# A burst of forty identity transpositions ahead of the first tokens, and token tiles transposed one by one as they are normalised

## The chip, the cores and the metric

One Trainium2 chip, one core of it. The metric is the device time of one execution in microseconds (us), median of the runs.

## What is computed

A graph-attention layer and a mixture-of-experts layer, each on layer-normalised tokens with a residual, over 16 batches of 512 tokens of 256 features in fp32. Cut to what matters:

```python
q, k, v = xn @ Wq.T, xn @ Wk.T, xn @ Wv.T          # xn = layernorm(x), 8 heads of 32
scores = where(adj != 0, q k^T / sqrt(32), -inf)
c = softmax(scores) @ v
gate = sigmoid(concat(c, xn) @ Wg.T + bg)
x = x + gate * xn + (1 - gate) * c
x = x + sum over the top 2 of 8 experts, and a shared expert, of (silu(y Wg) * (y Wu)) Wd     # y = layernorm(x)
```

## The kernel before, in words

**Two phases, one order of slots.** Attention runs first, the experts behind it; `seam` (L53) is the order of the work for TensorE, ScalarE and VectorE. Attention goes through iterations b = -1, 0, ..., 17 of 32 slots each. A slot is one score tile: one head's 128 queries against 512 keys. TensorE does the score matmul (L532, into one of two PSUM banks `S`), VectorE scales, masks and takes the row maximum (L916), ScalarE exponentiates (L677), TensorE transposes the result in four 128x128 tiles (L543), ScalarE or, in two slots of each 32, VectorE copies that to SBUF (L665, L908), and every eight slots TensorE multiplies by v (L576). Iteration b does the scores of batch b; between the slots' own work stand "units" of other batches' work, by the table `UNIT_AT` (L25).

**Units.** P0 and P1 (slots 18 and 19) transpose the normalised tokens of batch B = b+1: `turn` (L439) makes four transpositions of 128x128 (L441), one for each tile of 128 tokens, for one half of the features. ScalarE copies the bank to a rounded high part (`xt_h`, L605) and VectorE makes the rest (`xt_l`, L769). Q0 and K0 (slots 22, 23 and 24, 25, one half of the contraction in each) multiply by the weights, as three matmuls each time (`split`, L433: high x high, high x low, low x high; L435, L436, L437), and L611 and L772 take the result apart in the same way. Q1, K1, V0, V1 follow in the next iteration. A unit's bank is free again when the counter `g_free` says so; the units pass in one order, those that an iteration does not need being passed by with a bare increment.

**The start.** In iteration -1 there are no scores. SP issues the loads (L337 to L344: the tokens of batch 0, the weights; then the first half of the adjacency, L366). VectorE takes the statistics of batch 0, GpSimd the reciprocal deviation (L1032), and VectorE normalises tile by tile in `first_batch` (L748, L755), each of the four instructions counting `s_xn` up by one. For every later batch GpSimd does that (L1037), in slot 13 of the iteration before. TensorE's program begins with a wait for the constants that GpSimd writes (`s_const`, L431; the last is `tok_i`, L1003), the identity among them, and its first work is P0. The wait before a P unit asks for all four tiles:

```python
                if name[0] == "P":
                    pe.wait_ge(s_xn, B * NT + NT)
                    last = turn(o, xn, k)
```

ScalarE rounds both halves of the q, k, v weights (L646, L647) ahead of its copy of P0, and the gate's weights (L649) behind that of P1. VectorE makes the weights' low parts (`split_qkv`, L713), each ahead of the low part of P0 and of P1, then turns the first half of the adjacency into a mask (`scores_mask`, L745). SP waits for that mask, loads the second half of the adjacency into the same tile (L395), waits for K0's low part and then issues twelve copies of the heads' rows into `stack` (L332), the store of the normalised tokens (L426) and the next loads. VectorE turns the second half into a mask three slots behind K0, and only then passes by the last units of iteration -1. That frees the counter on which Q1, K1, V0 and V1 of batch 0 wait; TensorE does those four at the end of iteration -1 (L553), and VectorE copies V1 (L780), works through `prepare` (L716 to L737) and takes the first score tile. TensorE is two score tiles ahead and then waits for it.

Of the kernel before, what the change touches and what calls it, by code (L numbers as in the profile page):

```python
# [6 lines left out]
P = 128  # L7
# [18 lines left out]
           "Z3": 17, "P0": 18, "P1": 19, "Q0": 22, "K0": 24, "X0": 29, "X1": 30}  # L26
HALVES = "QKV"

ACT_AT = {"exp": 5}
TURNED_BY_VECTOR = (14, 22)  # L30
DVE_AT = {"choose": 3, "mark": 4, "weigh": 6, "place": 14, "stat": 12, "var": 12, "bias0": 4, "bias1": 16, "gate": (17, 19),
# [41 lines left out]
def attention_phase(nc, sems, held, banks, x, adj, wqkv, wgate, bg, router_w, xn_dram, x1_dram, xt2_dram, xg_dram,  # L73
# [8 lines left out]
    NT = N // P  # L82
# [17 lines left out]
    if True:  # L100
        def sb(name, shape, dt=F32):
            return held.enter_context(nc.sbuf_tensor(name, shape, dt))

        def sem(name):
            return sems.enter_context(nc.semaphore(name))

        S = banks[0:2]
# [10 lines left out]
        xn = sb("xn", [P, NT, D])  # L118
# [74 lines left out]
        s_xn = sem("s_xn")  # L193
# [78 lines left out]
        def late(b):  # L272

            return b >= 2 if isinstance(b, int) else True

        def unit(b, name):

            return (b + 1) * NU + ORDER.index(name)

        def bank(b, name):  # L280
            if b >= NB:
                return banks[(SEAM_BANKS if b == NB else LAST_BANKS)[name]]
            return G[unit(b, name) % 3]
# [39 lines left out]
        def first(b):  # L323

            return isinstance(b, int) and b == -1
# [103 lines left out]

        def tensor(pe):  # L430
            pe.wait_ge(s_const, 9)  # L431

            def split(out, lh, ll, rh, rl, first, last):  # L433

                pe.matmul(out, lh, rh, start=first, stop=False)  # L435
                pe.matmul(out, lh, rl, start=False, stop=False)  # L436
                return pe.matmul(out, ll, rh, start=False, stop=last)  # L437

            def turn(out, src, kf):  # L439
                for i in range(NT):  # L440
                    last = pe.transpose(out[:, P * i:P * i + P], src[:, i, P * kf:P * kf + P], ident[:, :])  # L441
                return last

            def do_unit(b, par, name, piece, end):
                B, A = b + 1, b - 1
                o = bank(b, name)
                k = int(name[1])
                s = par

                if piece == 0 and not (isinstance(b, int) and b == -1 and ORDER.index(name) < 2):  # L450
                    if b == NB + 1 and name != "R0":
                        pe.wait_ge(g_free, unit(NB, LAST_BEHIND[name]) + 1)
                    elif b == NB + 1:
                        pe.wait_ge(g_free, unit(b, LAST_BEHIND[name]) + 1)
                    elif b == NB and name in SEAM_BEHIND:
                        pe.wait_ge(g_free, unit(b, SEAM_BEHIND[name]) + 1)
                    elif b < NB:
                        pe.wait_ge(g_free, unit(b, name) - 2)
                    elif name == "L0":
                        pe.wait_ge(g_free, unit(b, name) - 1)  # L460
                if name[0] == "P":
                    pe.wait_ge(s_xn, B * NT + NT)
                    last = turn(o, xn, k)
                elif name[0] in "QK":
                    if first(b):
                        pe.wait_ge(s_lo, piece + 1)
                    if k == 0:
                        pe.wait_ge(g_free, unit(b, f"P{piece}") + 1)
                    xs = s if k == 0 else 1 - s
                    c0 = (D if name[0] == "K" else 0) + P * k  # L470
                    last = split(o[:, :], wqkv_h[:, piece, c0:c0 + P], wqkv_l[:, piece, c0:c0 + P],
                                 xt_h[xs][:, piece, :], xt_l[xs][:, piece, :], piece == 0, piece == KF - 1)
                elif name[0] == "V":
                    i = 2 * k + piece
                    for kf in range(KF):
                        last = split(o[:, D * piece:D * piece + D], xt_h[1 - s][:, kf, P * i:P * i + P],
                                     xt_l[1 - s][:, kf, P * i:P * i + P], wqkv_h[:, kf, 2 * D:],
                                     wqkv_l[:, kf, 2 * D:], kf == 0, kf == KF - 1)
                elif name[0] == "C":
                    pe.wait_ge(s_norm, A * 2 + 2)  # L480
                    last = turn(o, c_tok, k)
                elif name[0] == "Z":
                    if isinstance(b, int) and b == 1:
                        pe.wait_ge(s_set, 7)
                    tok = slice(P * k, P * k + P)
                    pe.matmul(o[:, 0:D], pick2[:, :], bg2[:, :], start=True, stop=False)
                    for kf in range(KF):
                        split(o[:, 0:D], xt_h[s][:, kf, tok], xt_l[s][:, kf, tok],
                              wg_h[:, KF + kf, :], wg_l[:, KF + kf, :], False, False)
                    for kf in range(KF):  # L490
                        pe.wait_ge(g_free, unit(b, f"C{kf}") + 1)
                        last = split(o[:, 0:D], ct_h[:, kf, tok], ct_l[:, kf, tok],
                                     wg_h[:, kf, :], wg_l[:, kf, :], False, kf == KF - 1)
                elif name[0] == "X":
                    pe.wait_ge(s_xn2, A * NT + NT)
                    last = turn(o, xn2, k)
                elif name[0] == "L":
                    zt = z[:, :, :].rearrange("p i d -> p (i d)")
                    for kf in range(KF):
                        pe.wait_ge(g_free, unit(b - 1, f"X{kf}") + 1)  # L500
                        for i in range(NT):
                            last = pe.matmul(o[DK * i:DK * i + DK, 0:P], rw_wide[:, kf, :],  # L502
                                             zt[:, N * kf + P * i:N * kf + P * i + P], start=kf == 0, stop=kf == KF - 1)
                elif name[0] == "M":
                    pe.wait_ge(g_free, unit(b, "L0") + 1)
                    last = pe.transpose(o[:, 0:P], lgt[:, :], ident[:, :])
                elif name[0] == "R":


                    pe.wait_ge(s_rt, (b - 2) * RT + RT_MB)  # L510
                    oe = o[:, 0:NT * E].rearrange("p (i e) -> p i e", e=E)
                    pe.matmul(oe, below[:, :], mb[:, :, :], start=True, stop=False)
                    for j in range(NT - 1):
                        pe.matmul(oe[:, j + 1:NT, :], ones_b[:, :],
                                  mb[:, j:j + 1, :].to_broadcast([P, NT - 1 - j, E]), start=False, stop=False)
                    last = pe.matmul(oe, ones_b[:, :], msum[:, :].rearrange("p (o e) -> p o e", o=1)
                                     .to_broadcast([P, NT, E]), start=False, stop=True)
                if end:
                    last.then_inc(g_full, 1)

            def at(b, p):
# [24 lines left out]
                for name, piece, end in pieces(b, p):  # L546
                    if has(b, name, att, pre, post):
                        do_unit(b, par, name, piece, end)
                    elif end:

                        pe.wait_ge(g_full, unit(b, name))
                        pe.nop().then_inc(g_full, 1)
                if first(b) and p == POS - 1:  # L553

                    par0, att0, pre0, post0 = flags(0)
                    for name in EARLY:
                        if has(0, name, att0, pre0, post0):
                            for piece in range(2):
                                do_unit(0, par0, name, piece, piece == 1)
                        else:  # L560
                            pe.wait_ge(g_full, unit(0, name))
                            pe.nop().then_inc(g_full, 1)
# [28 lines left out]
        def scalar(act):  # L591
# [44 lines left out]
            def second_choice(A):  # L636

                act.wait_ge(s_rt, A * RT + RT_DL)
                act.activation(el[:, :], dl[:, :], ACT.Exp).then_inc(s_el, 1)

            def at(b, p):
# [38 lines left out]
                if was and ep % 16 == 0:  # L680
# [5 lines left out]
                    act.activation(ct[g][:, :], C[:, :], ACT.Copy).then_inc(s_ct, 1)  # L686
                if p == ACT_AT["exp"] and late(b):
                    second_choice(b - 2)
# [299 lines left out]
        def pool(pool):  # L988
# [32 lines left out]
            def at(b, p):  # L1021
# [33 lines left out]
                if post and p == POOL_AT["xn2"]:  # L1055
# [11 lines left out]
                    for h in range(2):  # L1067
                        pool.tensor_copy(xs_half[:, :, XW * h:XW * h + D], xn2_half[:, :, :, h]).then_inc(s_halves, 1)
            return at, scatter

        return Attention(sync, tensor, scalar, vector, pool, unit, RT, s_done, t_free, t_full, pv, s_rt, g_full, g_free,
                         s_st, s_ref, s_xnst)

# [829 lines left out]
```

## Time and profile before

| what | value |
|---|---|
| runs | 1725.0, 1723.13 and 1724.4 us, median 1724.4 us |
| the profiled execution | 1724.81 us; its span from first to last instruction 1723.1 us |
| TensorE matmul busy | 1679.2 us, 97% of the span |
| VectorE, ScalarE, GpSimd busy | 1294.6, 1085.8 and 666.9 us |
| mean granted TensorE clock | 0.995 |

PE is TensorE's matmul side, PEld its weight load, DVE VectorE, ACT ScalarE, POOL GpSimd, SPq the issue of DMAs by SP. A line L441 is line 441 of the kernel. In the timeline a row has its start in us, its length in us (of several instructions together where it says x4), and in brackets how long the engine had been idle and what ended that.

### The profile page before, as it was taken

The page shows a single profiled execution, that of the slowest core. Times are in us where ns is not written, and L with a number is a line of the kernel's source. Part 1 is how long each engine was busy: PE and PEld are TensorE (multiplying, and loading weights), DVE is VectorE, ACT ScalarE, POOL GpSimd, SP SyncE. Part 2 cuts the span into 40 slices and gives each one's busy share as a digit, 9 for nine tenths or more (in the row PEclk, how much of TensorE's full clock was granted, in tenths as well). Part 3 has the DMA queues.
Part 4 walks back from the last instruction along what each step waited for, and adds up shares of the span by engine and source line. Part 5 has one row for each costly group of instructions (what it writes and reads, how often), then busy time and mean ns, then how long its engine had stood idle before and what let it go on. Part 6 is the DMA issues. An engine that isn't in the chain of part 4 may idle for free.

```text
span 1723.1 us, 35527 instructions
## 1 busy us (share of the span) xinstructions
PE 1679.2 (97%) x12185; PEld 1417.9 (82%) x12185; DVE 1294.6 (75%) x3220; ACT 1085.8 (63%) x2477; POOL 666.9 (39%) x512
## 2 busy tenths in 40 slices
PE   5999999999999999999999999999999999999997
PEld 4778888777887877887788888888898889888986
DVE  5688888888888888888555554777878787878784
ACT  4898888989888898988534333344444444434443
POOL 0146554456645445663331000034333443343334
PEclk9999999999999999999999999999999999999999
DMA  7355566656556665556333345587977786888773
GB/s 192 102 148 154 165 176 173 180 161 169 157 169 175 170 181 165 164 153 177 100 134 111 110 150 197 147 178 144 164 171 172 163 165 151 172 174 174 142 165 41
DMA packets 228081, 269.50 MB, mean 156 GB/s; under 512 B 107200, under 2 KB 184384, under 8 KB 222912
## 3 DMA queue, kind: packets, MB, share of 16 engines
q1 hardware_dynamic: 201312, 231.31, 50.2%
q0 software_dynamic: 26592, 35.93, 11.2%
q8 instruction: 99, 1.62, 0.4%
q14 instruction: 78, 0.64, 0.1%
HBM read 123.38 MB, written 74.86 MB: 115 GB/s over the span
## 4 chain that ended last, share of the span: by engine, by line
PE 45%; issue 1%; DVE 1%; DMA 1%; POOL 1%; ACT 1%; POOLq 0%; DVEq 0%; ACTq 0%
PE bank L1418 15%; PE bank L1420 15%; PE bank L1419 15%; DMA out_x<-yb,ix 1%; POOL out_x L1292 1%; DVE am L1587 0%; DVE wh L1547 0%; ACT ah L1513 0%; DVE xl L1578 0%; ACT yb L1501 0%; DVE al L1590 0%; ACT xh L1487 0%; PE bank L441 0%; DVE wa L1617 0%; PE bank L502 0%
## 5 line engine op out<-in xcount | busy, mean ns | idle before, releaser
L916 DVE CUSTOM_DVE_ANT_0 pf<-bank,bias_q 128x512 f32<-128x512 f32 x512 | 348.9, 687 | 130.2 <-PE bank L532 125.5
L1292 POOL DMA_INDIRECT out_x<-yb,ix x142 | 237.1, 1670 | 536.0 <-ACT yb L1501 409.9
L1513 ACT ACTIVATE ah<-am 128x512 fp32r<-128x512 f32 (+1 forms) x220 | 133.0, 605 | 424.7 <-DVE am L1587 424.7
L677 ACT ACTIVATE pf<-pf,nmax 128x512 f32<-128x512 f32 x512 | 373.7, 730 | 21.2 <-DVE nmax L916 21.2
L1418 PE MATMUL bank<-xh,wh 128*128 128x512 f32 (+1 forms) x880 | 334.4, 380 | 1.5 <-ACT pt L665 0.9
L1420 PE MATMUL bank<-xh,wl 128*128 128x512 f32 (+1 forms) x880 | 332.6, 378 | 0.0
L1419 PE MATMUL bank<-xl,wh 128*128 128x512 f32 (+1 forms) x880 | 332.5, 378 | 0.0
L543 PE MATMUL bank<-ident,pf 128*128 128x128 f32 x2048 | 312.6, 275 | 8.2 <-DVE pt L908 4.2
L543 PEld LDWEIGHTS bank<-ident,pf 128*128 128x128 f32 x2048 | 251.8, 141 | 64.6 <-issue 21.4
L665 ACT ACTIVATE pt<-bank 128x512 f32<-128x512 f32 x480 | 288.0, 600 | 10.3 <-PE bank L543 8.6
L1590 DVE TENSOR_TENSOR al<-am,ah 128x512 fp32r<-128x512 f32 (+1 forms) x220 | 146.7, 667 | 147.6 <-ACT ah L1513 147.6
L532 PE MATMUL bank<-stack 96*128 96x512 f32 x512 | 234.4, 458 | 5.8 <-DVE nmax L916 5.0
L1418 PE MATMUL bank<-wh,ah 128*128 128x256 f32 x824 | 232.6, 282 | 1.5 <-issue 1.5
L1420 PE MATMUL bank<-wh,al 128*128 128x256 f32 x824 | 232.6, 282 | 0.0
L1419 PE MATMUL bank<-wl,ah 128*128 128x256 f32 x824 | 232.6, 282 | 0.0
L1587 DVE TENSOR_TENSOR am<-sg,bank 128x512 f32<-128x512 f32 (+1 forms) x220 | 142.7, 649 | 81.6 <-PE bank L1420 78.0
L1418 PEld LDWEIGHTS bank<-xh,wh 128*128 128x128 f32 x880 | 165.5, 188 | 36.8 <-issue 3.8
L1420 PEld LDWEIGHTS bank<-xh,wl 128*128 128x128 f32 x880 | 165.3, 188 | 32.4
L1419 PEld LDWEIGHTS bank<-xl,wh 128*128 128x128 f32 x880 | 165.4, 188 | 29.8
L1017 POOL DMA_INDIRECT xg_dram<-xs,idx x128 | 132.9, 1038 | 107.8 <-DVE idx L892 60.9
L1511 ACT ACTIVATE sg<-bank 128x512 f32<-128x512 f32 (+1 forms) x220 | 124.2, 565 | 77.3 <-PE bank L1420 75.7
L1418 PEld LDWEIGHTS bank<-wh,ah 128*128 128x128 f32 x824 | 157.0, 190 | 3.6 <-issue 1.6
(209 smaller groups left out, 3050.6 us busy)
## 6 DMA issues: line engine op xcount, KB each, us to landing
raw<-in_w_all SPq DMA_DIRECT2D x39, 1536.0 KB, 7.5
stack<-qk SPq DMA_DIRECT2D x384, 128.0 KB, 2.4
adj_i<-in_adj SPq DMA_DIRECT2D x32, 512.0 KB, 4.7
xn<-in_x SPq DMA_DIRECT2D x16, 512.0 KB, 6.2
xn_dram<-xn SPq DMA_DIRECT2D x16, 512.0 KB, 2.9
xp<-in_x SPq DMA_DIRECT2D x16, 512.0 KB, 7.0
xnp<-xn_dram SPq DMA_DIRECT2D x16, 512.0 KB, 7.9
x_dram<-x SPq DMA_DIRECT2D x16, 512.0 KB, 3.2
```

The source lines that it names most:

```text
L532: pe.matmul(S[p % 2][:, :], stack[0:SR, hd, 0, P * tq:P * tq + P], stack[0:SR, hd, 1, :], start=True, stop=True).then_inc(s_full, 1)
L543: last = pe.transpose(T[ep % 2][:, P * kt:P * kt + P], pf[ep % RING][:, P * kt:P * kt + P], ident[:, :])
L665: act.activation(pt[r][:, j, :, P * (tq % 2):P * (tq % 2) + P], T[ep % 2][:, :].rearrange("p (k q) -> p k q", q=P), ACT.Copy).then_inc(t_f ...
L677: act.activation(pf[i][:, :], pf[i][:, :], ACT.Exp, bias=nmax[:, i:i + 1], scale=-1.0, accum_out=den[:, g, tq, j:j + 1]).then_inc(p_exp, 1)
L916: dve.tensor_tensor_reduce(pf[r][:, :], S[p % 2][:, :], bias_q[1 - par][:, tq, :], -SCALE, -3.0 * MASKED, ALU.add, ALU.min, nmax[:, r:r + ...
L1292: pool.indirect_dma_start(out=out, out_offset=bass.IndirectOffsetOnAxis(ap=ix[n % RING][:, i:i + 1], axis=0), in_=yb[s][:, i, :], in_offse ...
L1418: pe.matmul(out_, lh, rh, start=first, stop=False)
L1419: pe.matmul(out_, lh, rl, start=False, stop=False)
L1420: return pe.matmul(out_, ll, rh, start=False, stop=last)
L1513: act.activation(ah[s][:, m, 0:cols], am[m % 2][:, 0:cols], ACT.Copy).then_inc(s_ah, 1)
L1587: dve.tensor_tensor(am[m % 2][:, 0:cols], sg[m % 2][:, 0:cols], UB[m % 2][:, 0:cols], ALU.mult).then_inc(s_am, 1)
L1590: dve.tensor_tensor(al[s][:, m, 0:cols], am[m % 2][:, 0:cols], f32(ah[s][:, m, 0:cols]), ALU.subtract).then_inc(s_al, 1)
```

## The change

TensorE's program transposes the identity 40 times into the first score bank, once the constants are there and before anything else; the bank is written by the first score matmul later on. `turn` can take a start count: with it, each of the four transpositions of a P unit waits for its own tile of normalised tokens, not the first of them for all four. All P units of all batches are issued in this way. Nothing else differs.

```diff
+WARM = 40
...
         def tensor(pe):
             pe.wait_ge(s_const, 9)
+            for _ in range(WARM):
+                pe.transpose(S[0][:, 0:P], ident[:, :], ident[:, :])
...
-            def turn(out, src, kf):
+            def turn(out, src, kf, ready=None):
                 for i in range(NT):
+                    if ready is not None:
+                        pe.wait_ge(s_xn, ready + i + 1)
                     last = pe.transpose(out[:, P * i:P * i + P], src[:, i, P * kf:P * kf + P], ident[:, :])
                 return last
...
                 if name[0] == "P":
-                    pe.wait_ge(s_xn, B * NT + NT)
-                    last = turn(o, xn, k)
+                    last = turn(o, xn, k, B * NT)
```

## Rows read from the trace of the kernel before

**Rows 1.** Busy by stretch: us, then PE, PEld, DVE, ACT, POOL, granted clock, DMA share, GB/s
```profile
0.00:50.00 50.00, 30.16 (x171) 22.18 (x171) 31.56 (x87) 27.34 (x60) 9.14 (x21) 0.97 0.61 166
...
100.00:200.00 100.00, 99.14 (x881) 80.26 (x880) 82.93 (x266) 89.41 (x221) 45.81 (x37) 1.00 0.57 159
```

**Rows 2.** Timeline, the first 12 us: start, length, engine, line, operation, idle before
```profile
2.54 0.12 POOL L1003 IOTA tok_i<- 128x4 int32 x1
...
8.58 1.38 DVE L755 TENSOR_SCALAR xn<-xn,mv,rstd 128x256 f32<-128x256 f32 x4 [1.23 <-POOL rstd L1032]
...
10.10 0.83 ACT L647 ACTIVATE wqkv_h<-diff 128x768 fp32r<-128x768 f32 x1
10.11 1.94 PE L441 MATMUL bank<-ident,xn 128*128 128x128 f32 x8 [10.11 <-DVE xn L755]
...
11.23 0.60 ACT L605 ACTIVATE xt_h<-bank 128x512 fp32r<-128x512 f32 x1 [0.31 <-PE bank L441]
```

**Rows 3.** Timeline, 12 to 20 us, on TensorE, ScalarE, VectorE and SP
```profile
12.70 0.77 PE L435 MATMUL bank<-xt_h,wqkv_h 128*128 128x512 f32 x1 [0.65 <-DVE xt_l L769]
...
14.17 0.77 PE L435 MATMUL bank<-xt_h,wqkv_h 128*128 128x512 f32 x1
...
14.65 0.37 SPq L395 DMA_DIRECT2D adj_i<-in_adj  x1
...
15.58 0.63 PE L435 MATMUL bank<-xt_h,wqkv_h 128*128 128x512 f32 x1
...
16.01 0.56 PE L436 MATMUL bank<-xt_l,wqkv_h 128*128 128x512 f32 x1
...
16.64 0.40 PE L435 MATMUL bank<-xt_h,wqkv_h 128*128 128x512 f32 x1
...
17.11 0.39 PE L437 MATMUL bank<-xt_h,wqkv_l 128*128 128x512 f32 x1
...
18.16 0.69 DVE L772 TENSOR_TENSOR qk<-bank,qk 128x512 fp32r<-128x512 f32 x1 [1.02 <-ACT qk L611]
18.77 0.68 DVE L745 TENSOR_SCALAR bias_q<-adj_i 128x1024 bf16<-128x1024 int32 x1
...
19.10 0.50 PE L435 MATMUL bank<-xt_h,wqkv_h 128*128 128x512 f32 x1 [1.60 <-ACTq L634]
```

**Rows 4.** DMA issues of 14.7 to 18.5 us: KB each, us from issue to landing
```profile
adj_i<-in_adj SPq DMA_DIRECT2D x1, 512.0 KB, 3.3
```

**Rows 5.** Timeline, 25 to 30 us, on VectorE and TensorE
```profile
25.02 0.69 DVE L780 COPY v<-bank 128x512 f32<-128x512 f32 x1 [0.75 <-PE bank L437]
...
28.55 0.69 DVE L916 CUSTOM_DVE_ANT_0 pf<-bank,bias_q 128x512 f32<-128x512 f32 x1 [0.36 <-DVE bg L733]
...
29.39 0.47 PE L532 MATMUL bank<-stack 96*128 96x512 f32 x1 [3.94 <-DVE nmax L916]
```

**Rows 6.** Busy by stretch again, columns as in the first group
```profile
10.10:12.10 2.00, 1.94 (x8) 1.55 (x8) 1.20 (x2) 1.44 (x4) 0.00 (x0) 1.00 0.03 9
29.90:33.30 3.40, 3.24 (x12) 2.73 (x13) 2.41 (x9) 3.28 (x10) 0.00 (x0) 0.52 0.71 226
33.30:50.20 16.90, 13.35 (x102) 9.06 (x101) 13.19 (x40) 16.05 (x41) 6.29 (x5) 1.00 0.59 141
50.40:53.80 3.40, 3.40 (x16) 3.04 (x15) 0.70 (x2) 2.35 (x6) 0.00 (x0) 0.51 0.46 159
```

**Rows 7.** Timeline, TensorE and GpSimd, 43 to 53 us
```profile
43.62 0.60 PE L543 MATMUL bank<-ident,pf 128*128 128x128 f32 x4
...
44.80 5.28 POOL L1037 TENSOR_SCALAR xn<-xn,mv,rstd 128x256 f32<-128x256 f32 x4 [0.22 <-POOL rstd L1032]
...
50.23 0.84 PE L441 MATMUL bank<-ident,xn 128*128 128x128 f32 x4 [1.04 <-POOL xn L1037]
```

**Rows 8.** PE's score matmuls of 50.4 to 53.8 us: busy us, mean ns, then idle before
```profile
L532 PE MATMUL bank<-stack 96*128 96x512 f32 x2 | 1.6, 775 | 0.0
```

**Rows 9.** PE's token transpositions, 60 us to the end, same columns
```profile
L441 PE MATMUL bank<-ident,xn 128*128 128x128 f32 x240 | 36.0, 273 | 0.0
```

## The prediction

> **What bounds the kernel now.** I read the busy time by stretch first. From 100 to 200 us TensorE is busy for 99.14 of 100 us; in the first 50 us for 30.16 [rows 1]. So TensorE sets the pace nearly everywhere, and what it loses it loses in the start: the reader is to see that 20 of the profile's 44 idle us lie there, and that time won in the start is kept, since a shift of the first score tile moves a full TensorE behind it. The second view is the timeline of the start, for the chain that leads to the first score tile. Batch 0's four tiles are normalised from 8.58 to 9.96 us, TensorE does its eight transpositions from 10.11 to 12.05, ScalarE takes P0 at 11.23 [rows 2]. Q0 begins at 12.70, its second half at 14.17, K0's last matmul ends at 17.50, its low part at 18.85. VectorE then makes the second mask (18.77) and Q1 can start at 19.10, TensorE having been idle for 1.60 us [rows 3]. V1's copy, VectorE's preparations and the first score tile at 28.55 follow without slack [rows 5].
>
> The third view is TensorE's clock. The column of granted clock says 1.00 for 10.1 to 12.1 us [rows 6], but no change had been recorded by then; the spacing of like matmuls tells the level. From 15.58 to 16.01 it is 0.43 us a matmul, from 16.64 to 17.11 it is 0.235 for each of two [rows 3]: the low level (1.2 GHz) up to about 16.2, the high one (2.4 GHz) after. The clock is low again from 29.9 to 33.3 (0.52) and from 50.4 to 53.8 (0.51) [rows 6], once behind 3.94 us of idle [rows 5], once behind 1.04 us [rows 7].
>
> **The burst.** It can start when the constants are there, at 2.66 us [rows 2]. Four transpositions at the high level take 0.60 us [rows 7] and one lasts 0.27 [rows 9], so the step is (0.60 - 0.27) / 3 = 0.11 us; at the low level eight take 1.94 [rows 2], a step of 0.22 with the last one's 0.42 behind seven of them. Forty at the low level are 8.8 us, up to 11.5; at the high level 4.4. When would the clock rise? The trace shows it rising 3.5 us after Q0's first matmul and 6.1 us after the first transposition [rows 2, 3]; these are my two ends. After 3.5 us 16 transpositions are done, and 24 x 0.11 = 2.6 us end the burst at 8.9; after 6.1 us 28 are done, and 12 x 0.11 = 1.3 us end it at 10.2. Both fit under the work of VectorE and GpSimd that fills this time anyway, so I cost the burst at nothing; without that cover it costs the time by which P0 becomes late (the third rival).
>
> **P0 and P1 tile by tile.** The first tile is ready at about 8.9, the last at 9.96. With the burst over by then, P0 needs one more transposition and ends at about 10.3; with the burst over at 10.2 it ends at 10.8. Before, it ended at 11.2. But ScalarE is rounding weights until 10.93 [rows 2], so its copy of P0 moves from 11.23 to 10.93 and the part is worth 0.30 us, not 0.9. P0's low part, the weights' second low part and P1's low part follow each other on VectorE and move by the same 0.30: Q0 starts at 12.4, its second half at 13.87.
>
> **Q0 and K0 at the high level.** From Q0's second half to the end of K0 there are nine matmuls. At 0.235 us each, with 0.1 for the first and 0.39 for the last one's length [rows 3], they take 8 x 0.235 + 0.5 = 2.4 us and end at 16.2 instead of 17.50, 1.3 earlier. K0's low part ends 1.35 us behind them in the rows, so at 17.6. What is late next is the second half of the adjacency: SP issues its load at 14.65, behind the first mask, which moves by 0.30 only, to 14.35; it lands 3.3 us later [rows 3, 4], at 17.65, and VectorE's second mask begins there instead of at 18.77. That is 1.1 us, and Q1 to V1, VectorE's preparations and the first score tile shift by it. SP's twelve copies into `stack` wait for K0's low part and start 1.3 us earlier, so SP's queue (the store, the loads for batch 1) is not the late one. In the slots that follow ScalarE is busy for 16.05 of 16.9 us [rows 6] and keeps its pace, so the 1.1 us pass through.
>
> **The waits in later batches.** For batch 1 GpSimd normalises until 50.08 and TensorE stands 1.04 us before its four transpositions [rows 7]. Three of them now run inside that wait: 3 x 0.11 = 0.33 us less. From 60 us on the token transpositions had no idle time in front of them [rows 9]. They get 6 more waits a batch, 90 in 15 batches. A wait that is already met stood between P0 and P1 at 10.11, and the eight took 1.94 us in one piece [rows 2], nothing to be seen to 0.01 us; so 0 to 0.9 us, below zero excluded; I take 0.
>
> **The sum.** -1.1 - 0.3 = -1.4 us. The profiled execution took 1724.8 us, its span and 1.7 around it, and stands 0.4 over the median of 1724.4; the sum gives 1723.4 for it and 1723.0 for the median.
>
> **Whether a transposition counts as activity.** Of the 16 matmuls from 50.4 to 53.8 two are score matmuls and the other 14 transpositions, and the clock comes back at the end of that stretch [rows 6, 8], so here transpositions seem to raise it; no row shows a stretch of them alone.
> The Trainium skill ("TensorE: Matmul & The Clock Gate", "Part 4: PE-mode transpose") says the opposite, that the full clock does not engage for work in transpose mode because it does not count as busy in the same way. By that rule the burst would stay at the low level and the sum would be the third rival's; the rows bear it out only so far as none excludes it.
>
> **Rivals.** First, the expected chain: 1723.0, chance 0.45.
> Second, the clock rises in the burst and falls before it is of use. TensorE is idle from about 11.2 to 12.4, and again between Q0's halves. For it: the fall at 50.4 came behind 1.04 us of idle in a half-filled stretch [rows 6, 7]. Against: 1.60 us of idle ahead of 19.10 brought none [rows 3, 6]. With all nine matmuls at 0.43 they take 4.2 us and K0 ends at 18.05, 0.55 later than now; with some of them high, up to 0.3 earlier. With the 0.33 of batch 1 off: 1723.8 to 1724.6, so 1724.2, chance 0.20.
> Third, on the other side: the burst does not raise the clock and holds P0 up. It ends at 11.5, P0 at 11.5 + 3 x 0.22 + 0.42 = 12.6 against 11.2; ScalarE's copy, Q0 and the rest come 1.4 us later. It decides from the point where the burst ends after 10.6 (high level) or 10.1 (low). 1724.4 + 1.4 - 0.3 = 1725.5, chance 0.15.
> Fourth, the low stretch at 50.4 is gone, because the tokens of batch 1 keep TensorE busier or the clock's own timing falls otherwise. In that stretch TensorE is busy for all 3.40 us at half speed, but ScalarE for 2.35 [rows 6], which then bounds it: 3.40 - 2.35 = 1.05 us less, 1722.0, chance 0.15. The same price turned round (a low stretch that is new) and whatever else has 0.05.
>
> **The numbers.** The prediction is the first case, 1723.0. The range goes from 1721.2, which takes in the fourth case and 0.8 us of scatter (the three runs lie within 1.9 us), to 1725.8, which takes in the third and 0.3. A measurement of this kernel tells 0.2%, 3.4 us, from no change; every case lies inside that. Faster by more would need the first and the fourth together and about a microsecond beyond: 0.03. Slower by more needs a burst held up and two new low stretches, or a price for the 90 waits four times my bound: 0.02. Same: 0.95.
>
> **What would show it.** In the profile of the changed kernel 40 transpositions should start at 2.7 us with a step of 0.22 that falls to 0.11 after 3.5 to 6 us, and end between 8.9 and 10.2; ScalarE's copy of P0 should start at 10.9, Q0's matmuls be 0.235 us apart, the second mask begin at 17.7 behind the adjacency's load, and the first score tile at 27.4. The burst's step staying at 0.22 would prove the third case, Q0 and K0 at 0.43 the second. A first score tile more than 2 us earlier, or a shift there that is not found again at 60 us, would prove the chain wrong.

## The result, and the profile after

The changed kernel is slower: 1727.4 us median of 9 runs (1726.2 to 1729.7) against 1723.4 of 9 (1722.4 to 1725.0), a ratio of 1.0024, 95% interval 1.0015 to 1.0032, so 2.6 to 5.5 us. A second set of 11 runs on one chip gave 1726.97 against 1723.16, ratio 1.0022 (1.0013 to 1.0031). The profiled execution took 1727.28 us, its span 1725.6; the one of before was 1724.81 and 1723.1, so these two profiles differ by 2.5 us. In the sets below one execution of the kernel before (2038.5 us) and one of the kernel with the burst moved (2063.1 us) ran at a mean granted clock of 0.76 and 0.75, and are left out of every figure.

Busy by stretch, the changed kernel, same columns as [rows 1]:

```profile
0.00:50.00 50.00, 35.56 (x202) 27.65 (x202) 28.67 (x82) 24.38 (x53) 6.00 (x19) 0.93 0.59 166
100.00:200.00 100.00, 99.16 (x881) 80.31 (x880) 82.83 (x265) 89.48 (x222) 44.96 (x37) 1.00 0.57 159
```

TensorE is busier in the first 50 us, by the burst, while VectorE and ScalarE have each done about 3 us less by then. From 100 to 200 us nothing changed. So the loss is in the start. Its timeline, where [rows 2] and the first of [rows 3] stood:

```profile
2.72 7.45 PE L434 MATMUL bank<-ident 128*128 128x128 f32 x40 [2.72 <-POOL tok_i L1007]
...
9.09 1.40 DVE L808 BATCH_NORM_STATS2 stats<-xn 128x6 f32<-128x256 f32 x4 [7.68 <-PEq L556]
9.51 1.28 ACT L650 ACT_TABLE_LOAD   x1 [9.51 <-ACTq L638]
...
12.45 1.38 DVE L759 TENSOR_SCALAR xn<-xn,mv,rstd 128x256 f32<-128x256 f32 x4 [1.23 <-POOL rstd L1036]
...
13.01 1.64 PE L446 MATMUL bank<-ident,xn 128*128 128x128 f32 x8 [2.85 <-DVE xn L759]
...
14.25 1.08 ACT L609 ACTIVATE xt_h<-bank 128x512 fp32r<-128x512 f32 x2 [1.87 <-PE bank L446]
...
15.72 0.76 PE L438 MATMUL bank<-xt_h,wqkv_h 128*128 128x512 f32 x1 [1.07 <-DVE xt_l L773]
...
17.66 0.37 SPq L396 DMA_DIRECT2D adj_i<-in_adj  x1
...
21.56 0.69 DVE L749 TENSOR_SCALAR bias_q<-adj_i 128x1024 bf16<-128x1024 int32 x1
...
31.33 0.69 DVE L920 CUSTOM_DVE_ANT_0 pf<-bank,bias_q 128x512 f32<-128x512 f32 x1 [0.36 <-DVE bg L737]
```

The burst itself did what was forecast: from 2.72 to 10.17 us. But the second row shows VectorE's statistics of batch 0 starting only at 9.09, after 7.68 us of idle time that is put down to `PEq L556`, TensorE's sequencer. In the kernel before they started at 5.22:

```profile
5.22 1.41 DVE L804 BATCH_NORM_STATS2 stats<-xn 128x6 f32<-128x256 f32 x4 [3.82 <-DMA xn<-in_x]
```

There it was the tokens' own load that ended the wait. L556 (L552 before) is the bare increment of `g_full` by which TensorE passes by a unit that an iteration does not need. Thirteen of them stand ahead of P0 in iteration -1. Here they are, in the view of one line (engine, operation, count, lengths in ns, first and last start in us), before and after:

```profile
L552 PEldq EVENT_SEMAPHORE  x13: 51/51/51, 2.7 to 4.5; - x13
```

```profile
L556 PEldq EVENT_SEMAPHORE  x13: 51/51/51, 7.5 to 9.3; - x13
```

VectorE and ScalarE go through the same table of slots. Each passes by the same units, each time waiting for TensorE's increment (`skip`, `pass_by`), and VectorE comes to `first_batch` in slot 15 of iteration -1, behind those of the first units. TensorE's increments stand behind the burst in its program. So normalising the tokens, under which the burst was meant to be hidden, waits for the burst.

The shift along the chain: statistics +3.87 us, tokens +3.87, ScalarE's copy of P0 +3.02 (the tile by tile transpositions give 0.85 back), second mask +2.79, first score tile +2.78. The clock rose at 8.6 us, inside the burst, and had fallen again at 15.4, before Q0 began:

```profile
15.50:18.80 3.30, 3.08 (x7) 2.19 (x8) 2.14 (x4) 0.78 (x1) 0.00 (x0) 0.50 0.02 5
```

A granted clock of 0.50 is the low level, from 15.4 to 18.9 us. TensorE had been idle for 2.85 us ahead of P0 and for 1.07 ahead of Q0. So the high clock that the burst had brought was gone when Q0 began. K0, but for its first matmul, ran at the high level again and ended at 20.29, 2.79 us later than before.

### The profile page after: what moved, and what is told of

Its sections match the earlier page's. It is cut to its first block and busy times, and to the rows that moved or that the text cites. A ratio compares the mean times of both kernels' runs of the same rounds, so it can differ in the third digit from the quotient of the medians.

```text
span 1725.6 us, 35607 instructions
## 1 busy us (share of the span) xinstructions
PE 1685.3 (98%) x12225; PEld 1423.1 (82%) x12225; DVE 1294.9 (75%) x3220; ACT 1086.5 (63%) x2477; POOL 664.6 (39%) x512
## 5 line engine op out<-in xcount | busy, mean ns | idle before, releaser
L681 ACT ACTIVATE pf<-pf,nmax 128x512 f32<-128x512 f32 x512 | 373.9, 730 | 21.2 <-DVE nmax L920 20.3
```

Of the source, the lines that this page charges most:

```text
L681: act.activation(pf[i][:, :], pf[i][:, :], ACT.Exp, bias=nmax[:, i:i + 1], scale=-1.0, accum_out=den[:, g, tq, j:j + 1]).then_inc(p_exp, 1)
```

## The experiments

Each is told by its difference to the changed kernel. Where a mean is given, it is over a kernel's timed runs; the 80 of the kernel before average 1723.9 us and scatter by 1.2 (standard deviation), so a single run says little below 2 us. "Statistics" are VectorE's first work on batch 0's tokens, the first score tile is its first one (L916 before).

**The two parts apart.** First the tile waits alone:

```diff
-            for _ in range(WARM):
-                pe.transpose(S[0][:, 0:P], ident[:, :], ident[:, :])
```

> Burst taken out, tile by tile waits kept. Theory A (the bare increments with which TensorE passes by the units of iteration -1 stand behind the burst, and VectorE's first_batch waits for them): VectorE's statistics start at 5.2 us as before the change, ScalarE's copy of P0 at 10.9, the first score tile near 28.2; 0.3 to 0.7 us less than the kernel before. Rival B (the additional waits of the P units cost time on TensorE): 1 to 4 us more than before.

Measured: 1723.16 us against 1724.21, ratio 0.9990 (0.9981 to 0.9998), 1.0 us less (1.2 in the means) where I had said 0.3 to 0.7. Its start in the timeline:

```profile
5.16 1.41 DVE L806 BATCH_NORM_STATS2 stats<-xn 128x6 f32<-128x256 f32 x4 [3.76 <-DMA xn<-in_x]
...
9.09 2.20 PE L444 MATMUL bank<-ident,xn 128*128 128x128 f32 x8 [9.09 <-DVE xn L757]
...
10.14 0.83 ACT L649 ACTIVATE wqkv_h<-diff 128x768 fp32r<-128x768 f32 x1
10.87 1.06 ACT L607 ACTIVATE xt_h<-bank 128x512 fp32r<-128x512 f32 x2
```

Transpositions begin 1.0 us earlier, ScalarE's copy only 0.36 earlier, right behind its rounding of the weights; the first score tile is at 28.39, 0.16 earlier. Rival B falls: the 90 added waits cost nothing that shows. Then the burst alone:

```diff
                 if name[0] == "P":
-                    last = turn(o, xn, k, B * NT)
+                    pe.wait_ge(s_xn, B * NT + NT)
+                    last = turn(o, xn, k)
```

> Burst kept, the old wait for all four tiles. Theory A: statistics start at 9.1 us as after the change, P0 starts at 13.9, and the time is 4 to 5 us over the kernel before, so up to 1 us over the changed kernel. Rival B: within 1 us of the kernel before.

Measured: 1728.93 us against 1724.21, ratio 1.0025 (1.0015 to 1.0035); the mean lies 4.6 us over that of before. Statistics at 8.35, P0 at 13.24. In this run the clock rose at 5.9 us, so the burst was shorter than in the changed kernel, and both came a little sooner than I had said. The whole loss, and more, is the burst's. The changed kernel, with both parts, loses less than this one.

**The same burst behind the increments.**

```diff
-            for _ in range(WARM):
-                pe.transpose(S[0][:, 0:P], ident[:, :], ident[:, :])
...
+                if first(b) and p == UNIT_AT["P0"]:
+                    for _ in range(WARM):
+                        pe.transpose(S[0][:, 0:P], ident[:, :], ident[:, :])
                 for name, piece, end in pieces(b, p):
```

> The same forty transpositions and waits, the burst moved behind the increments of slots 0 to 17, right ahead of P0. Theory A: statistics start at 5.2 us again, the burst runs from about 3.5 to 11, the first score tile comes between 27.4 and 29, and the time is within 1 us of the kernel before. Rival C (the burst costs wherever it stands, because the eight real transpositions come behind it or because it leads the clock into a fall): 2 to 4 us over the kernel before.

Measured: 1725.7 us against 1724.21, ratio 1.0006 (0.9997 to 1.0015). Timeline of TensorE and VectorE:

```profile
4.66 5.86 PE L550 MATMUL bank<-ident 128*128 128x128 f32 x40 [4.66 <-PEq L557]
4.98 1.41 DVE L809 BATCH_NORM_STATS2 stats<-xn 128x6 f32<-128x256 f32 x4 [3.57 <-DMA xn<-in_x]
```

The same forty transpositions, and VectorE waits for its DMA again. Most of the loss is gone: Theory A, in its main point, is shown. Not all of it went: the mean lies 1.2 us over that of before, just outside the 1 us of Theory A and below the 2 to 4 of Rival C. The burst now runs until 10.5, ScalarE takes P0 at 11.04, not later than before, but the clock fell once more:

```profile
12.49 0.47 PE L436 MATMUL bank<-xt_h,wqkv_h 128*128 128x512 f32 x1 [1.10 <-DVE xt_l L774]
12.80 0.39 PE L437 MATMUL bank<-xt_l,wqkv_h 128*128 128x512 f32 x1
13.03 0.39 PE L438 MATMUL bank<-xt_h,wqkv_l 128*128 128x512 f32 x1
13.96 0.57 PE L436 MATMUL bank<-xt_h,wqkv_h 128*128 128x512 f32 x1 [0.54 <-DVE xt_l L774]
14.33 0.63 PE L437 MATMUL bank<-xt_l,wqkv_h 128*128 128x512 f32 x1
14.76 0.63 PE L438 MATMUL bank<-xt_h,wqkv_l 128*128 128x512 f32 x1
```

Q0's first half has steps of 0.23 us, the high level; from 14.2 the steps are 0.43, behind 1.10 and 0.54 us of idle time. Here the clock fell though the burst had delayed nobody. It was low until 17.6, into K0's last matmul, where before the record has it rise at 16.4, and the first score tile came 0.34 us later than before.

**The burst's length.** With `WARM = 20`:

> The change with 20 transpositions in the burst, at its old place. They take 20 x 0.217 = 4.4 us and end at 7.3. Theory A: the increments come about 1 us ahead of that, statistics start between 6.2 and 7.0 us, and the time is 1 to 2 us over the kernel before. Rival C: P0 is not late at all here (its tiles are ready at 10 at the earliest), so the time is that of the kernel before within 0.5 us.

Measured: 1724.36 against 1724.21, ratio 1.0001 (0.9992 to 1.0010). I was wrong on the size: statistics at 4.97, no later than before, and the first score tile at 28.32, where it was with the tile waits alone (28.39). The time is as Rival C had it, and by the time alone the two could not be told apart here; that the loss is VectorE's wait is read from the statistics of the longer bursts. The mean is still 1.2 us over that of the tile waits alone on the same chip (1724.3 and 1723.1), which the start does not show. And with `WARM = 60`:

> The change with 60 transpositions. Theory A: the increments come with the 43rd transposition, 2.2 to 2.8 us later than in the changed kernel, VectorE's statistics start between 10.6 and 11.9, and the time is 6.0 to 7.0 us over the kernel before. Rival C (only the part of the burst that overlaps P0 costs): the same or more, but with VectorE's statistics at 5.2.

Measured: 1728.83 against 1723.49, ratio 1.0030 (1.0018 to 1.0042), mean difference 5.1 us; statistics at 11.48, first score tile 5.4 us later. The statistics came when Theory A had said, and not at 5.2 as Rival C had it; the time is 1 us below Theory A's 6.0 to 7.0. The increments of the two, 20 ahead of 60:

```profile
L556 PEldq EVENT_SEMAPHORE  x13: 51/51/51, 3.2 to 5.0; - x13
```

```profile
L556 PEldq EVENT_SEMAPHORE  x13: 51/51/51, 9.9 to 11.8; - x13
```

In the traces the first increment follows 0.02 us behind the start of a transposition's weight load: the 4th of 20, the 24th of 40 and the 44th of 60. So TensorE's sequencer had 16 whole transpositions handed over that the array had not begun, each time. The burst costs VectorE nothing up to the length whose increments end by the time the tokens have landed, and what is above that comes on top: statistics at 4.97, 9.09 and 11.48 us for 20, 40 and 60. The step from 40 to 60, 2.4 us here, is twenty transpositions mostly at the high level.

**Fillers in the gaps to the end of K0.** If the clock falls because of the gaps, fillers in them should bring what the chain promised. In the expectations this kernel is e5_kept:

```diff
-WARM = 40
+WARM = 20
+GAPS = {("P0", 0): 12, ("Q0", 0): 14, ("Q0", 1): 6}
...
                 for name, piece, end in pieces(b, p):
+                    if first(b):
+                        for _ in range(GAPS.get((name, piece), 0)):
+                            pe.transpose(S[0][:, 0:P], ident[:, :], ident[:, :])
```

> Burst of 20 at the old place (the increments of iteration -1 come 17 transpositions ahead of the engine, so it holds nobody up), 12 more right ahead of P0, 14 between P1 and Q0, 6 between Q0's halves, so that TensorE is never idle from 2.7 us to the end of K0. Theory A with the clock as the second part: Q0 and K0 at 0.235 us a matmul, K0 ends near 16.3, the first score tile near 27.5, 1.5 to 2.5 us less than the kernel before. Rival D (the clock is worth nothing here, the adjacency's load or VectorE bounds the chain): the first score tile at 28.2 to 28.4 and the time of the kernel with the tile waits alone, about 1 us less than before. If the clock stays low the fillers take double and Q0 comes 1 us later than there.

Its chain to the first score tile:

```profile
13.83 0.47 PE L439 MATMUL bank<-xt_h,wqkv_h 128*128 128x512 f32 x1
...
15.73 0.39 PE L441 MATMUL bank<-xt_h,wqkv_l 128*128 128x512 f32 x1
...
17.89 0.69 DVE L753 TENSOR_SCALAR bias_q<-adj_i 128x1024 bf16<-128x1024 int32 x1 [0.41 <-DMA adj_i<-in_adj]
...
27.60 0.69 DVE L924 CUSTOM_DVE_ANT_0 pf<-bank,bias_q 128x512 f32<-128x512 f32 x1 [0.36 <-DVE bg L741]
```

The kernel with the same 20 transpositions and no fillers is the one to hold it against. Stretches of the two, columns as in [rows 1], first without and then with fillers:

```profile
9.60:16.20 6.60, 5.37 (x15) 3.74 (x16) 3.94 (x7) 3.89 (x6) 0.00 (x0) 0.50 0.17 48
```

```profile
6.10:26.40 20.30, 15.24 (x96) 12.47 (x94) 12.30 (x29) 6.31 (x10) 1.05 (x1) 1.00 0.56 155
```

Without fillers the clock rose at 6.1 us and was low from 9.5 to 16.3; with them it stayed at the high level from 6.0 to 26.5 us, though TensorE was still idle for 1.2 of the 13.3 us from 2.7 to 16.0. K0 ended at 16.1 instead of 17.5, and then the second mask waited for the adjacency's load, the first time in any of these kernels that this load is what is late. The first score tile is 0.95 us earlier. That is the chain of the prediction with its arithmetic. The time did not follow: 1723.18 against 1723.49, ratio 0.9996 (0.9987 to 1.0005), where I had said 1.5 to 2.5 us less. It is the time that Rival D gave, with the first score tile of Theory A. In both profiles of this kernel the low stretch around 30 us is 6.8 us long (26.5 to 33.3 here), where it is 3.4 in those of the tile waits alone; whether that takes back what was won is not shown.

The next kernel adds to the fillers 30 transpositions in front of batch 0's third score matmul.

```diff
+                    if isinstance(b, int) and b == 0 and p == 2:
+                        for _ in range(30):
+                            pe.transpose(T[1][:, 0:P], ident[:, :], ident[:, :])
                     if not isinstance(b, int) or b > 0 or p >= 2:
                         pe.wait_ge(s_done, n - 1)
```

> As e5_kept, and 30 transpositions more between the second and third score matmul of batch 0, where TensorE is idle for 3.9 us. Theory A: the low stretch at 30 us is gone, 0.3 to 0.6 us less than e5_kept. Rival D: no difference, because ScalarE sets the pace of these slots.

```profile
26.27 5.16 PE L537 MATMUL bank<-ident 128*128 128x128 f32 x30 [1.44 <-DMA stack<-qk]
31.18 0.72 PE L540 MATMUL bank<-stack 96*128 96x512 f32 x2
```

1724.23 against 1723.49, ratio 1.0001 (0.9992 to 1.0010), 1.0 us over the kernel with fillers alone in the means: neither theory. The filler stood behind the wait for the third head's copy, started late, ran in part at the low level (a stretch that began at 26.4 us) and left the third score matmul 1.8 us later than before, at 31.18 against 29.39 [rows 5]. The same fault as the burst's, at another place: a filler longer than its gap.

**Once more on one chip**, the kernel with the tile waits alone, the one with fillers, and the changed kernel. A second profile of the changed kernel had come before:

> The changed kernel once more, for a second profile: statistics at 9.0 +- 0.7, the first score tile 2.8 to 3.8 us later than before, as the clock rises earlier or later in the burst.

Statistics at 8.72, first score tile at 31.89, 3.34 us later than before; 1728.78 us. Then the three, timed:

> The tile waits alone once more, beside the next two on one chip. Theory A: 0.5 to 1.5 us less than the kernel before.

> The kernel of e5_kept once more. Theory A (a start 0.8 us shorter than with the tile waits alone is kept to the end): 0.5 to 1 us less than e9_tiles_again. Rival D (what is won ahead of the first score tile is lost on the way): the same as e9_tiles_again or more.

> The changed kernel once more, timed. Theory A, with the two profiled starts of it 2.8 and 3.3 us later than before and the rest unchanged: 2.8 to 4.0 us over the kernel before.

| kernel | median us | before | ratio, 95% interval |
|---|---|---|---|
| tile waits alone | 1722.98 | 1723.16 | 0.9997 (0.9987 to 1.0006) |
| fillers | 1722.69 | 1723.16 | 0.9996 (0.9987 to 1.0005) |
| changed kernel | 1726.97 | 1723.16 | 1.0022 (1.0013 to 1.0031) |

With the first sets the tile waits alone average 1722.8 us over 22 runs, the fillers 1723.1 over 22, the changed kernel 1727.3 over 20, the kernel before 1723.9 over 80. The changed kernel's loss, in the means of each set, is 4.0 and 3.5 us. Both of the first two are clearly better than the changed kernel; against the kernel before they win about 1 us, which lay beyond the interval in one of two sets for the tile waits, and in neither for the fillers. On the one chip the fillers' mean is 0.5 us over that of the tile waits alone, as Rival D had it and not Theory A. That their 0.8 us at the first score tile is kept to the end could not be shown.

## Why the prediction was wrong

The time lies outside the range, on the side that had 0.15 and by another mechanism than the one named there.

**The step that failed** is in the part on the burst: "Both fit under the work of VectorE and GpSimd that fills this time anyway, so I cost the burst at nothing". I took the time of that work from the rows and did not ask what the work itself waits for. No row before showed the dependence, since the tokens' load ended the wait there, but the code does: thirteen increments behind the burst, and VectorE and ScalarE pass by the same units one by one. The cover was not independent of what it should cover. In place of 0 the term is 2.9 to 3.5 us at the first score tile: it came 2.78, 3.34 and 3.31 us later than before in three profiles of the changed kernel, and 0.16 earlier with the tile waits alone. From the forecast of -1.4 us to the measured 3.5 to 4.0 there are about 5 us: these 2.9 to 3.5, the 1.1 us of the clock, which was not to be had (below), and about 1 us that is not traced.

**The third rival** was right that the burst could be the cause and gave 1725.5, but by P0 standing behind a burst that stays at the low level. The burst ended at 10.17, inside its bounds of 8.9 to 10.2; P0 was not late because TensorE was busy, it was late because its tokens were.

**The second rival came true as well**: the clock rose in the burst (at 8.6 us, and at 5.9 to 7.9 in others) and was low again from 15.4 to 18.9, for all of Q0 and K0's first matmul (from 13.5 to 20.3 in the two other profiles of the changed kernel). So the 1.1 us of the first case were not to be had. With fillers they nearly were: 0.95 at the first score tile. So the chain's own terms held: ScalarE's copy of P0 forecast at 10.93 (10.87 with the tile waits alone), the second mask at 17.65 behind the adjacency (17.89 with the fillers), the first score tile at 27.4 (27.60).

**The wait for batch 1's tokens** gave about what was said (0.33 us). In the profile of the burst alone, which keeps the old wait, the last of the four transpositions ends at 54.80, 0.77 us behind GpSimd's last tile; with the tile waits alone it ends at 50.15, 0.38 behind it:

```profile
54.17 0.63 PE L446 MATMUL bank<-ident,xn 128*128 128x128 f32 x4 [1.04 <-POOL xn L1042]
```

```profile
49.82 0.33 PE L444 MATMUL bank<-ident,xn 128*128 128x128 f32 x1 [0.62 <-POOL xn L1039]
```

**The fourth rival's low stretch** at 50.4 us is in none of the other twelve profiles. With the tile waits alone, and with the burst alone:

```profile
50.40:53.80 3.40, 3.40 (x45) 2.15 (x43) 2.00 (x5) 3.40 (x9) 0.00 (x0) 1.00 0.47 159
```

```profile
36.80:60.00 23.20, 18.92 (x161) 13.16 (x160) 16.25 (x48) 20.98 (x53) 6.29 (x5) 1.00 0.51 134
```

In the first, 45 matmuls instead of 16, at the high level. But the second has the old wait and the same 1.04 us of idle time in front of batch 1's transpositions as before [rows 7], and no low stretch either. So that the tile waits took it away is not shown. It does mean that the profiled execution of before had a low stretch that the others lack, so the 2.5 us between the two profiles understate the loss, and the 3.5 to 4.0 us of the runs are its better size.

**The shift behind the first score tile.** The prediction asked whether it is found again at 60 us. Between the kernel before and the changed one it is 2.78 us at the first score tile and 1.26 at the 32nd (69.62 and 70.88 us), with the low stretch of before in between. Against the tile waits alone, which lack that stretch too, it is 2.94 and 3.47. In the profiles of the two from one chip, 3.39 us at the first tile are 4.02 at the 32nd and 4.24 in the span. So the shift is kept, and some of the further 1 us (4.5 us between the two in the means) comes before 70 us; what makes it is not traced. The mean granted clock of the runs, 0.9938 with the burst and 0.9960 with the tile waits alone, does not decide it: it counts the clock as high until its first recorded change, at 16.4 us without a burst and at 5.9 to 8.6 with it, so the low stretch of Q0 counts in the one and not in the other. With 20 transpositions the mean clock is 0.9935, and the time is that of the kernel before.

**Transpositions and the clock.** The Trainium skill ("TensorE: Matmul & The Clock Gate", "Part 4: PE-mode transpose") says that the full clock does not engage for transpose-mode work. The runs decide against it for the fp32 transpositions of this kernel: in a burst of nothing but fp32 transpositions the step fell from 0.21 to 0.11 us while it ran, in all ten profiles that have one, and the granted clock recorded the rise.

## What to carry to other kernels

Before filler work is put in front of an engine's program, list every semaphore increment that stands behind it, bare ones too, and ask whether the work that is to hide the filler waits for one of them, on however long a way. Idle time of an engine is a cover only if it ends by something that does not depend on that engine. And raising an engine's clock by filler work brought the chain forward here only where the gaps between the filler and the work were filled as well, each by no more than its length; what the chain won then ended where a load became late, here the adjacency's, and of it nothing could be shown in the kernel's time.

## What the runs showed of the hardware

A stream of transpositions lets TensorE's sequencer run 16 of them (a weight load and a matmul each) ahead of the array: with 20, 40 and 60 in the stream, the next instruction that is not one of them, an increment, ran 0.02 us behind the start of the weight load of the 4th, the 24th and the 44th. A bare increment behind a wait takes it 0.15 us, so thirteen of them take 1.9 us (7.5 to 9.3), and the burst that stood behind them started at 4.66 instead of 2.72. And in the run with the burst behind the increments the clock fell behind 1.10 and 0.54 us of idle time around three matmuls, where the kernel before kept it over 1.60 us of idle [rows 3].
